# Two accumulating transfers issued before, instead of after, four tile scalings on GpSimd

## The reference

```python
q_emb = relu(q @ W3 + b3)                       # 64 x 1024, a few small matmuls
x2 = (n * v + v.sum(axis=1)) * q_emb[:, None]   # scaling per channel, with the token sum
out = v + relu(x2 @ W2 + b2)                    # W2 is 1024 x 1024: nearly all of the work
```

## Time and profile before

| | |
|---|---|
| time, median of three runs | 633.65 us (633.63 to 634.02) |
| the profiled execution | 635.33 us, with a span of 633.5 us |
| TensorE busy | 626.5 us, 99% of the span |
| VectorE, ScalarE, GpSimd busy | 447.3, 415.8 and 27.3 us |
| granted TensorE clock | 1.00 |
| transfers | 112.05 MB, mean 177 GB/s |

### The profile page before, as it was taken

How to read it: one execution, slowest core, us unless ns; L and a number is a source line. 1 busy time by engine, 2 the same in 40 slices (tenths; PEclk the granted TensorE clock), 3 DMA queues, 4 the chain that set the end, 5 groups by cost and what they waited for, 6 DMA issues and landing times.

```text
span 633.5 us, 9163 instructions
## 1 busy us (share of the span) xinstructions
PE 626.5 (99%) x2791; PEld 516.8 (82%) x2791; DVE 447.3 (71%) x692; ACT 415.8 (66%) x889; POOL 27.3 (4%) x35
## 2 busy tenths in 40 slices
PE   9998999999999999999999999999999999999998
PEld 6886888888888888888888888888888888888886
DVE  4999799776776757677576776757677576776534
ACT  4976687939577594866839577494866939577320
POOL 1471100000000000000000000000000000000000
PEclk9999999999999999999999999999999999999999
DMA  8996648554353734347353353733347353350613
GB/s 329 390 315 173 164 164 307 193 200 143 143 179 132 255 143 133 133 164 232 132 199 132 141 190 132 248 149 124 141 166 232 132 197 127 147 193 1 225 42 132
DMA packets 27811, 112.05 MB, mean 177 GB/s; under 512 B 3088, under 2 KB 3600, under 8 KB 24208
## 3 DMA queue, kind: packets, MB, share of 16 engines
q1 hardware_dynamic: 26352, 107.43, 46.8%
q0 software_dynamic: 1152, 4.19, 3.5%
q10 hardware_dynamic: 288, 0.20, 0.1%
HBM read 78.25 MB, written 33.55 MB: 176 GB/s over the span
## 4 chain that ended last, share of the span: by engine, by line
PE 92%; DVE 4%; DMA 2%; ACT 1%; issue 1%; DVEq 0%
PE acc L359 91%; DMA u_sb<-w_q 2%; DVE w_lo L900 2%; PE acc L376 1%; ACT x_sb L519 0%; DVE vsum L783 0%; DVE a_lo L861 0%; ACT w_hi L546 0%; DVE x_sb L826 0%; ACT a_hi L505 0%; DVE x_sb L872 0%; DVE xn L905 0%; DVE scale L787 0%; DVE x_sb L881 0%; ACT acc L607 0%
## 5 line engine op out<-in xcount | busy, mean ns | idle before, releaser
L359 PE MATMUL acc<-w_hi,a_hi 128*128 128x512 f32 (+1 forms) x904 | 351.4, 389 | 3.0 <-DVE a_lo L861 2.9
L359 PE MATMUL acc<-w_lo,a_hi 128*128 128x512 f32 (+1 forms) x904 | 350.9, 388 | 0.0
L359 PE MATMUL acc<-w_hi,a_lo 128*128 128x512 f32 (+1 forms) x904 | 350.9, 388 | 0.0
L519 ACT ACTIVATE x_sb<-x_sb,bias,scale 128x128 f32<-128x128 f32 x476 | 196.7, 486 | 15.5 <-DVE bias L789 15.5
L359 PEld LDWEIGHTS acc<-w_hi,a_hi 128*128 128x128 f32 x904 | 169.8, 188 | 39.6 <-DVE a_lo L861 3.7
L359 PEld LDWEIGHTS acc<-w_hi,a_lo 128*128 128x128 f32 x904 | 169.8, 188 | 34.9
L359 PEld LDWEIGHTS acc<-w_lo,a_hi 128*128 128x128 f32 x904 | 169.8, 188 | 34.6
L895 DVE TENSOR_TENSOR a_lo<-x_sb,a_hi 128x512 fp32r<-128x512 f32 x140 | 96.6, 690 | 103.2 <-ACT a_hi L514 102.6
L514 ACT CAST a_hi<-x_sb 128x512 fp32r<-128x512 f32 x140 | 87.1, 622 | 37.5 <-PE acc L359 35.6
L514 ACT CAST a_hi<-s 128x512 fp32r<-128x512 f32 x56 | 34.8, 621 | 70.1 <-PE acc L359 68.7
L783 DVE TENSOR_REDUCE vsum<-x_sb 128x16 f32<-128x2048 f32 (+2 forms) x41 | 74.1, 1809 | 6.4 <-DMA x_sb<-x_t 6.4
(11 more groups left out here) (61 smaller groups left out, 242.5 us busy)
## 6 DMA issues: line engine op xcount, KB each, us to landing
xn<-x SPq DMA_DIRECT2D x64, 512.0 KB, 4.0
out<-xn SPq DMA_DIRECT2D x62, 512.0 KB, 3.1
x_sb<-x_t SPq DMA_DIRECT2D x28, 1024.0 KB, 5.0
x_sb<-x_t SPq DMA_DIRECT2D x7, 512.0 KB, 12.8
w_stage<-w_q POOLq DMA_DIRECT2D x6, 512.0 KB, 6.8
xn<-w_t SPq DMA_DIRECT2D x4, 512.0 KB, 6.0
u_sb<-w_q SPq DMA_DIRECT2D x2, 512.0 KB, 12.9
m_sb<-w_q SPq DMA_DIRECT2D x2, 512.0 KB, 14.2
```

Source lines behind the costliest of these rows:

```text
L359: return nc.tensor.matmul(dst, lhs, rhs, start=False, stop=False, skip_group_check=True)
L519: last = nc.scalar.activation(x_sb[:, slot, h, t, k], x_sb[:, slot, h, t, k], ACT.Identity, bias=bias[:, slot, h, t, k:k + 1], scale=scale ...
```

## The change

The loop that waits for a split and issues T1's two accumulating transfers moves on GpSimd's list. It stood behind the scaling of A12 and A22 of unit 0 and waited for B21's halves (counts 5 and 6); it stands ahead of them now and waits for B11's second and fourth piece (counts 2 and 4), which are the pieces that lie in the two halves of the buffer that it adds to.

```diff
             scale_tiles(0, A11, range(2, KH))
             scale_tiles(0, A21, range(1))
+            for h in range(2):
+                pool.wait_ge(w_lo_ready, split("b11", 2 * h + 1))
+                add_half(w_halves, 0, 1, h, t1_summed)
             scale_tiles(0, A12, range(KH))
             scale_tiles(0, A22, range(KH // 2))
-            for h in range(2):
-                pool.wait_ge(w_lo_ready, split("b21", h))
-                add_half(w_halves, 0, 1, h, t1_summed)
             scale_tiles(3, A21, range(KH))
```

## The result

The changed kernel takes 636.78 us (median of six runs, 636.22 to 637.15), the kernel before on the same chip 633.89 (633.63 to 634.84). The ratio is 1.0041, with a 95% interval from 1.0029 to 1.0054: slower by 1.8 to 3.4 us. The forecast was 637.5, slower by 3.9.

What follows compares the result with a forecast made beforehand. TensorE, busy 99%, bounds the kernel; VectorE's reaching the low part awaited at 58.74 sets the end. 5.0 lost by q1, less 0.55, 0.1 and 0.48, gives +3.9 on 633.65: 637.5 us, range 634.6 to 639.4.

Steps and rivals of the forecast that it cites:

- GpSimd's issue: GpSimd's two early issues, at about 14.3 and 15.6 us, cost nothing; 3.8 us of idle time are left before 20.32.
- the collision: VectorE's low part at 39.12 took 3.90 us beside GpSimd's subtraction; slipping past could save up to 2.6 us, counted as nothing.
- the matmul of 58.74: TensorE's matmul at 58.74 us, after which it never stops again; forecast to move to about 62.6.
- the prediction's own sign: Sign of being wrong: a late m_sb cast with the matmul of 58.74 less than 2 us later, meaning larger slack further on.
- The queue's loss: SyncE's queue q1 loses 5.0 us (bounds 4.8 and 5.3) to the accumulation, from about 18.5 to 27.1 us.
- the landing at 22.77 + 5.0 = 27.8: B21's second half bears q1's whole loss and lands at 27.8 us instead of 22.77.
- The slack, 0.55 + 0.1 + 0.48 us: Taken off the 5.0: 0.55 at ScalarE's cast, 0.1 at the next low part, 0.48 at VectorE's wait for B22.
- TensorE's standstill: TensorE stands still 3.6 us from 26.55, waiting for the low part of B21's second half; swallowed by later gaps.
- The clock: Rival: TensorE's clock falls after its standstill; 637.5 to 637.7 us, or 639.4 with a stretch twice as long; chance 0.11.
- B22's landing: B22's first half, landed at 38.02 us, should not move, as the same transfer work is done by 38.
- The later start: Rival: accumulation's first packets at 20.5 us, not 18.5, giving 635.7 us; chance 0.12, shared with VectorE slipping past late.

Runs made afterwards that it cites:

- e2: Changed kernel with only T1's first transfer issued early, the second back at its old place waiting for B21's second half; 634.51 us, ratio 1.0006 to the kernel before.
- e3: Changed kernel with T1's two early transfers as plain copies of the same bytes instead of accumulations; 635.07 us, ratio 1.0014 to the kernel before.
- e4: Kernel before with SyncE issuing B21's second half three places later, T1's transfers at their old place on GpSimd's list; 635.80 us, ratio 1.0029.
- e7: Changed kernel with one subtraction of activations, s3(3), moved from GpSimd to a gap of VectorE; 635.45 us, ratio 1.0022 to the kernel before.
- e6: Kernel before with one subtraction of activations, s3(3), moved from GpSimd to a gap of VectorE; 632.41 us, ratio 0.9973.
- e5: Kernel before, unedited, run again for a third trace; 633.91 us, in the middle of the timed executions.
- e9: Kernel before with subtraction s3(3) on VectorE and T1's two transfers issued later, after the seventh activation quarter's low part; 632.02 us, ratio 0.9971.
- e10: Kernel before with subtraction s3(3) and the bias sum on VectorE, T1's transfers issued after the seventh activation quarter's low part; 631.26 us, ratio 0.9965.

## Why the prediction was right, point by point

**The mechanism held.** GpSimd's issue was free, the accumulation ran before 27 us, B21's second half was late, ScalarE idled for it, TensorE stopped once more, and the end moved. The wait grows with the time that the packets take, and the time with the wait:

| kernel | ScalarE's wait for B21's second half | time above its reference |
|---|---|---|
| e2, one accumulation early | 0.71 us | 0.40 us |
| e3, two copies early | 1.67 us | 0.96 us |
| e4, the half issued late | 2.65 us | 1.69 us |
| the change | 3.30 us | 2.89 us |
| e7 against e6 | 3.40 us | 3.04 us |

e3 speaks against the issue on GpSimd as the cause, e6 and e7 against the collision, and e4 shows that the lateness of this one load is enough. In e2, e3 and e4 the collision falls where it does in the changed kernel (a scale of 1.42 to 1.44 us), so only e7 against e6 is free of it.

**What was chance in the number.** The terms were read from an execution of 635.33 us and the sum put on the median. Against that execution the profiled one of the changed kernel (636.33) is 1.0 us longer, and the matmul of 58.74 comes 1.0 later; by the prediction's own sign, a late cast with this matmul less than 2 us later, it would have been wrong. Against e5, an execution at the median, both differ by 2.4 us (633.91 to 636.33, 57.31 to 59.73). A sum whose landing was 1.7 us off came out only 1.0 us off (3.9 against 2.9); that is in part luck, since the first trace's late start and long collision were chance.

**The queue's loss, forecast 5.0 us: right.** Between e6 and e7, the third unit's activations, which stand behind B21's second half, landed at 8.35 + 15.2 = 23.6 and 8.39 + 19.7 = 28.1, later by 4.5 us, with e7's queue 0.3 us ahead at the last transfer before the accumulation (18.3 against 18.6, B21's first half): 4.8 us. These are the rows of their issues, e6 and e7:

```profile
x_sb<-x_t SPq DMA_DIRECT2D x1, 512.0 KB, 15.2
```
```profile
x_sb<-x_t SPq DMA_DIRECT2D x1, 512.0 KB, 19.7
```

**The step that was mis-sized: the landing at 22.77 + 5.0 = 27.8; it was 26.1.** Two things make up the 1.7 us. The queue ran 0.7 us earlier than in the first trace with its late start (B21's first half landed at 18.0 against 18.7). And B21's second half did not bear the whole loss: from the landing of B21's first half to that of its second passed 4.1 us in the first trace and 8.1 in the changed kernel, 4.0 more (3.7 and 8.2 from e6 to e7, 4.5 more), and the rest of the loss came with the transfer behind it.

Besides, one trace could not tell the transfer's own time from what stood beside it. Halves of 512 KB land 1.3 us apart in this queue, but 2.8 us passed ahead of B21's second half in the first trace (20.0 to 22.8); in e5, the same kernel, it landed at 7.91 + 13.0 = 20.9, and a gap of 2.6 us came ahead of B12's first half (22.8 to 25.4). At both places the traces show one packet of 16 KB of the kind "instruction", here in the first trace from 20.4 to 20.6 us and in e5 from 22.5 to 22.8:

```profile
q8 instruction: 1, 0.02, 34.3%
```
```profile
q8 instruction: 1, 0.02, 23.0%
```

34.3% of sixteen engines over 0.2 us is 1.1 us of one engine. In all seven traces with the old place of T1's transfers or a later one and SyncE's list unchanged the gap stands at this packet: ahead of B21's second half where it runs at 19.7 to 20.5 us, ahead of B12's first half where it runs at 22.3 or 22.6 (e9, e5). That it makes the gap is likely, not shown. In the changed kernel and in e7 it runs at 19.9 and 19.8, ahead of B21's second half; how much of it is in the 26.1 stays open.

**The slack, 0.55 + 0.1 + 0.48 us: about right in size, not in each term.** The first term was chance: in e5 the half landed 2.1 us ahead of its cast. The cast's place in ScalarE's list is steadier, 22.9 to 23.3 in the three traces of before. From e5 to the changed kernel, ScalarE's cast is 3.1 us later (23.00 to 26.11), VectorE's next low part 3.0 (25.62 to 28.62), its low part of B22 2.9 (38.54 to 41.40), TensorE's resumption 2.4 (57.31 to 59.73). VectorE's own idle time before B22 was only 0.20 us in e5.

**The collision, counted at nothing with 2.6 us as the bound: right in effect.** VectorE of the changed kernel:

```profile
41.40 1.22 DVE L900 TENSOR_TENSOR w_lo<-u_sb,w_hi 128x1024 fp32r<-128x1024 f32 x1
42.53 1.39 DVE L900 TENSOR_TENSOR w_lo<-m_sb,w_hi 128x1024 fp32r<-128x1024 f32 x1
...
44.44 1.43 DVE L787 TENSOR_SCALAR scale<-q_emb 128x4 f32<-128x4 f32 x1
```

It slipped past, as the prediction allowed, and met a small scale instead (1.43 us against 0.15). The low part of 1.39 us is not from this subtraction, as it takes 1.40 in e7 too. The loss is thus 1.28 us; against e5 with 1.7 this is 0.4 us given back, against the first trace 1.3.

**TensorE's standstill, forecast 3.6 us, was 1.9,** for the same reason as the landing, and was swallowed by its later waits as forecast.

**The clock,** a rival of the prediction, falls in some executions, but at no cost that can be told. In the profiled execution of the changed kernel it stayed: granted 1.00, and the matmuls behind the standstill of 1.9 us are 0.23 us apart again from the second on. In e4, with a standstill of 1.77 us up to 27.95, it fell. TensorE of e4 in order of time, and its stretch from 30 to 31 us, with the granted clock in the third column from the right:

```profile
28.75 0.40 PE L359 MATMUL acc<-w_hi,a_hi 128*128 128x512 f32 x1
...
29.33 0.63 PE L359 MATMUL acc<-w_hi,a_lo 128*128 128x512 f32 x1
29.76 0.63 PE L359 MATMUL acc<-w_hi,a_hi 128*128 128x512 f32 x1
...
59.17 0.50 PE L359 MATMUL acc<-w_hi,a_hi 128*128 128x512 f32 x1 [0.73 <-DVE a_lo L861]
```
```profile
30.00:31.00 1.00, 1.00 (x3) 0.75 (x3) 0.82 (x4) 1.00 (x3) 0.00 (x0) 0.50 1.09 274
```

From 29.1 to 32.5 us the granted clock was 0.50, the lower of its two levels (1.2 of 2.4 GHz), and from 29.33 to 32.32 the matmuls were 0.43 us apart instead of 0.23, 1.6 us of TensorE's time in all. It was swallowed, as the rival's working has it: at 59.17 TensorE still waits 0.73 us for VectorE. The Trainium skill ("TensorE: Matmul & The Clock Gate", part 1) tells of a drop to the lower level after an idle time; e4 agrees with it. One of six executions of the changed kernel (636.71 us), one of six of e4 and one of eleven of e7 (635.55 us) have a mean granted clock of 0.997, and every other one of all kernels at least 0.999; their times lie among the others. The granted clock is no witness for the start: it reads 1.00 from 2 to 6 us of the first trace, where matmuls are 0.43 us apart.

**B22's landing** did not move later (37.0 us, against 38.0 in the first trace and 37.4 in e5), so the accumulation's time was indeed given back behind 27 us. **The later start** of the accumulation did not come: its first packets ran at 17.5 us, 4.3 behind the first issue, as before (29.2, behind 24.87).

## What to carry to other kernels

A transfer that is issued as soon as its buffer allows is not free when the queues are full: it takes its time from the loads that stand behind that moment, so ask which of them has the least slack. Issuing it behind the last load that something waits for gave the fastest version here (e10), though what the later issue alone gained is not shown. Price a transfer by the time that its packets hold the engines, from the queue's share, not by its bytes. And take a landing that decides the sum from more than one execution.

## What the runs showed of the hardware

- Accumulating transfers into on-chip memory held the DMA engines 5.25 us per 1.05 MB (61.1% of 8.6 us), a plain copy of the same bytes on the same queue 2.6 us (e3).
- A subtraction of 128 x 512 on GpSimd with both inputs in on-chip memory stretched a VectorE instruction beside it by 1.3 to 2.7 us, though it lists 1.9 us itself (lengths on GpSimd are rough in the profile); which instruction it hit differed between executions of one kernel. The Trainium skill ("SBUF — State Buffer", "SBUF: two separate sides") has the two engines share a port that one of them holds for a whole instruction, with the other fully blocked. The stretched low parts, and that the stretch went away when the subtraction left GpSimd (e6), agree with it; that a stretch can exceed the 1.9 us is not explained by it.
- The first matmul on loaded data came between 5.11 us and 6.30 us in executions with the same instructions up to there; the twelve matmuls ahead of it were 0.43 us apart for a stretch of varying length, all twelve where it came at 6.30, and 0.22 us apart behind that stretch.
- Behind a standstill of TensorE of 1.8 to 1.9 us the granted clock fell to 0.50 for a while in e4 (29.1 to 32.5 us), and not in the traces of the changed kernel and of e7.
- Between 18 and 26 us, in seven of seven traces without an early accumulation, the one landing of the plain queue that came late, by 0.9 to 1.5 us, stood at a 16 KB packet of the kind "instruction"; that the packet makes it late is likely, not shown.
